# GATv2 edge scores: products on VectorE, gathers written out, turned one-hots made on ScalarE

## The reference, cut to what matters

```python
x_l = (x @ W_l + b_l).reshape(n, H, C)      # n=6250, H=8, C=32
x_r = (x @ W_r + b_r).reshape(n, H, C)
x_j = x_l[src]
g = leaky_relu(x_r[dst] + x_j, 0.2)
alpha = einsum('ehc,hc->eh', g, att) + log(edge_attr)[:, None]
# ... softmax of alpha over the edges of each dst, out = segment_sum(x_j * alpha, dst)
```

## Time and profile before

| what | value |
|---|---|
| time of three runs | 5920.71, 5924.41, 5925.23 us; median 5924.41 |
| the profiled execution | 5924.94 us, its span 5923.2 us |
| busy over the span | PE 68%, DVE 44%, ACT 19%, POOL 52% |
| granted TensorE clock, mean | 0.749 of full speed |
| HBM traffic over the span | 104 GB/s |
| `score_edges` | from about 245 to 1546 us of the span |

### The profile page before, as it was taken

The page is one execution under the profiler, slowest core; times in us unless marked ns, Lnnn a source line. Parts: engine busy times, 40 slices in busy tenths (PEclk is TensorE's granted clock), DMA queues, the critical chain, the costliest instruction groups (busy, mean ns, idle before and its releaser), DMA issues. The chain is left out here.

```text
span 5923.2 us, 82263 instructions
## 1 busy us (share of the span) xinstructions
PE 4048.7 (68%) x19460; PEld 3300.3 (56%) x19461; DVE 2628.5 (44%) x5923; ACT 1112.7 (19%) x2524; POOL 3097.9 (52%) x3161
## 2 busy tenths in 40 slices
PE   4788999999469965089934555555455555592998
PEld 3577888888447744067734444444444444461665
DVE  5333333333689975034444434444433334342443
ACT  0122222222159921022210000000000000021121
POOL 1166767676248831500066777777677777603111
PEclk9889888888679985599955556666555555555999
DMA  5365555565248843342242111111211111122220
GB/s 197 94 183 182 180 178 181 177 181 177 70 157 273 272 135 108 122 125 64 62 122 54 32 32 33 33 33 30 44 33 32 33 32 34 28 72 81 84 79 31
DMA packets 414884, 602.72 MB, mean 102 GB/s; under 512 B 97612, under 2 KB 305118, under 8 KB 413351
## 3 DMA queue, kind: packets, MB, share of 16 engines
q1 hardware_dynamic: 283019, 348.08, 17.8%
q0 software_dynamic: 107056, 200.91, 14.7%
q10 hardware_dynamic: 24732, 52.87, 2.6%
HBM read 392.17 MB, written 221.97 MB: 104 GB/s over the span
## 5 line engine op out<-in xcount | busy, mean ns | idle before, releaser
L1867 POOL DMA_INDIRECT big<-t_d,src_tiles x1564 | 1497.9, 958 | 552.2 <-issue 462.5
L2090 PE MATMUL v_bank<-big,v_oh 128*128 x3328 | 682.9, 391 | 926.4 <-POOLq L1863 861.6
L2090 PEld LDWEIGHTS v_bank<-big,v_oh 128*128 128x128 f32 x3328 | 649.6, 299 | 1004.0 <-issue 1004.0
L640 POOL DMA_INDIRECT se_xj<-xl_d,se_idx x832 | 833.8, 1002 | 371.9 <-issue 193.0
L1945 DVE TENSOR_TENSOR big<-big,v_bank 128x64 f32 x1664 | 367.8, 221 | 1158.0 <-PE v_bank L2090 922.8
L737 PE MATMUL se_z_ps<-big,se_oht 128*128 x1664 | 543.4, 455 | 73.1 <-issue 45.7
L683 DVE TENSOR_TENSOR se_z<-se_z_ps,se_xj 128x528 f32<-128x528 f32 x416 | 293.3, 705 | 584.8 <-DMA se_xj<-xl_d,se_idx 450.3
L976 POOL TENSOR_TENSOR ae_v<-ae_v,ex 128x1792 f32<-128x1792 f32 x104 | 334.2, 3217 | 243.0 <-DMA ae_v<-xj_d 242.8
L759 PEld LDWEIGHTS se_al_ps<-atta,se_zt 128*128 128x128 f32 x3328 | 459.3, 214 | 0.0
L759 PE MATMUL se_al_ps<-atta,se_zt 128*128 128x8 f32 x3328 | 444.5, 260 | 0.0
L1017 PE MATMUL ae_bank<-ae_v,ae_oh 128*128 128x266 f32 x1664 | 401.1, 396 | 51.4 <-DVE big L1001 37.4
(11 more groups left out here) (406 smaller groups left out, 5916.6 us busy)
## 6 DMA issues: line engine op xcount, KB each, us to landing
xj_d<-se_xj SPq DMA_DIRECT2D x208, 528.0 KB, 3.4
ae_v<-xj_d SPq DMA_DIRECT2D x208, 528.0 KB
big<-t_d,src_tiles POOLq DMA_INDIRECT x1564
buf_d<-e_blank ACTq DMA_DIRECT2D x4, 4112.0 KB, 35.7
e_xs<-buf_d SPq DMA_DIRECT2D x106, 128.0 KB
y_d<-e_y SPq DMA_DIRECT2D x106, 128.0 KB
se_xj<-xl_d,se_idx POOLq DMA_INDIRECT x832, 3.1
v_xt<-xnt_d SPq DMA_DIRECT2D x98, 128.0 KB
```

Of the source, the lines that this page charges most:

```text
L640: nc.gpsimd.indirect_dma_start(half_of(u)[:, k, :], None, table, bass.IndirectOffsetOnAxis(ap=idx[:, u, k:k + 1], axis=0)).then_inc(landed ...
L1867: nc.gpsimd.indirect_dma_start(rows[:, t % RING, :], None, table, bass.IndirectOffsetOnAxis(ap=m.srct[:, t:t + 1], axis=0)).then_inc(lande ...
L2090: last = nc.tensor.matmul(bank[u][:, k * MH:(k + 1) * MH], oh[:, u, k, :], of_block(rows, at[k]), start=True, stop=True)
```

## The change

In `score_edges`:

- The gathers are written out: 832 instructions without a loop. Each reads its column of `m.src` itself; the copy into `idx` and the wait on it are gone. The half buffers are now a part of `m.big1`.
- PE only expands (L738 in the changed file). Turning the one-hot, turning the sum and the product with `m.atta` are gone, and `z_ps` has four buffers.
- DVE, for each pair, adds the rows (L685, as before), then computes max(z, 0) times 0.8 att in one instruction (L693, `weigh`; `attb` holds 0.8 att on each partition), and sums each 32 channels into `m.ex` (L698, `total`). Once a group it adds the linear part (L708). `project_nodes` makes `attl` with 0.2 in place of 0.6, since leaky_relu(z) is also 0.2 z + 0.8 max(z, 0).
- The turned one-hot is made directly: `edge_steps` copies `fl` to bfloat16 and stores it to DRAM (`dlr_d`), SP loads a group's 1024 destinations as one row broadcast to all partitions (`dlb`, 256 KB in SBUF), and ACT computes 1 - |destination - partition|, cut at 0, in two instructions of 128x1024 (L722, L724).

```diff
@@ edge_steps @@
-                sp.wait_ge(stored, 112)
+                sp.wait_ge(floats, 4)
+                sp.dma_start(m.dlr_d.rearrange("(j p) e -> p j e", p=P), flb[:, :, :]).then_inc(stored, 16)
+                sp.wait_ge(stored, 128)
...
+                dve.wait_ge(floats, 3)
+                nc.vector.tensor_copy(flb[:, :, :], fl[:, :, :]).then_inc(floats, 1)
@@ score_edges, POOL @@
-                    if at_least(h, 4):
+                for h in range(2 * NG):
+                    u, r = h % 4, h // 4
+                    if h >= 4:
                         pool.wait_ge(landed[u], 16 * HS * r)
                         pool.wait_ge(s["z_ready"], 2 * h - 6)
                         pool.wait_ge(stored[u], 16 * r)
-                    nc.gpsimd.tensor_copy(idx[:, u, :], m.src[:, bass.ds(h * HS, HS)]).then_inc(s["indexed"], 1)
-                    pool.wait_ge(s["indexed"], h + 1)
-                    pool.sem_inc(s["issued"], 1)
                     for k in range(HS):
+                        t = h * HS + k
                         nc.gpsimd.indirect_dma_start(half_of(u)[:, k, :], None, table,
-                                                     bass.IndirectOffsetOnAxis(ap=idx[:, u, k:k + 1], axis=0)).then_inc(landed[u], 16)
-                pipeline(pool, 2 * NG, 4, (0, gather))
+                                                     bass.IndirectOffsetOnAxis(ap=m.src[:, t:t + 1], axis=0)).then_inc(landed[u], 16)
@@ score_edges, SP @@
+                def load_locals(h, u, r):
+                    if u % 2:
+                        return
+                    g = 2 * r + u // 2
+                    if at_least(h, 4):
+                        sp.wait_ge(s["oh_apart"], g - 1)
+                    sp.dma_start(dlb[:, u // 2, :], m.dlr_d[bass.ds(g * GS, GS), :].rearrange("k e -> (k e)").partition_broadcast(P))\
+                        .then_inc(locals_in[u // 2], 16)
-                pipeline(sp, 2 * NG, 4, (0, store))
+                pipeline(sp, 2 * NG, 4, (0, load_locals), (4, store))
@@ score_edges, DVE @@
-                    nc.vector.tensor_tensor(z[:, u, k:k + 2, :], z_ps[v % 2][:, :, 0:LW], xj[:, u, k:k + 2, :],
+                    nc.vector.tensor_tensor(z[:, u, k:k + 2, :], z_ps[v % 4][:, :, 0:LW], xj[:, u, k:k + 2, :],
                                             ALU.add).then_inc(s["z_ready"], 1)
+                def weigh(q, v, r):
+                    u, k = v // GP, 2 * (v % GP)
+                    dve.wait_ge(s["z_ready"], q + 1)
+                    if at_least(q, 2):
+                        dve.wait_ge(s["totalled"], q - 1)
+                    nc.vector.scalar_tensor_tensor(w[:, v % 2, :, :], z[:, u, k:k + 2, 0:D], 0.0, wide,
+                                                   ALU.max, ALU.mult).then_inc(s["weighed"], 1)
+
+                def total(q, v, r):
+                    dve.wait_ge(s["weighed"], q + 1)
+                    nc.vector.tensor_reduce(m.ex[:, bass.ds(q * 2 * H, 2 * H)],
+                                            w[:, v % 2, :, :].rearrange("p k (h c) -> p (k h) c", h=H), AX.X, ALU.add)\
+                        .then_inc(s["totalled"], 1)
-                pipeline(dve, NS // 2, 2 * GP, (7, scores), (0, one_hot), (3, add))
+                pipeline(dve, NS // 2, 2 * GP, (0, add), (1, weigh), (2, total), (3, scores))
@@ score_edges, ACT @@
+                def spread(g, u, r):
+                    act.wait_ge(locals_in[u], 16 * (r + 1))
+                    if at_least(g, 2):
+                        act.wait_ge(s["z_made"], GP * (g - 1))
+                    row = oht[:, u, :, :].rearrange("p k n -> p (k n)")
+                    nc.scalar.activation(row, dlb[:, u, :], ACT.Abs, bias=place[:, 0:1], scale=-1.0).then_inc(s["oh_apart"], 1)
+                    act.wait_ge(s["oh_apart"], g + 1)
+                    nc.scalar.activation(row, row, ACT.Relu, bias=m.ones[:, 0:1], scale=-1.0).then_inc(s["oht_ready"], 1)
@@ score_edges, PE @@
-                pipeline(pe, NS // 2, 2 * GP, (0, turn_one_hot), (2, expand), (4, turn), (6, attend))
+                pipeline(pe, NS // 2, 2 * GP, (0, expand))
```

More of the change, by code:

```diff
@@ L609, in score_edges @@
         HS = GS // 2
-        idx = sb("idx", [P, 4, HS], U32)
-        xj = sb("xj", [P, 2, GS, LW])
+        xj = m.big1[:, CL:CL + 2 * GS * LW].rearrange("p (u k d) -> p u k d", u=2, k=GS)
         half_of = lambda u: xj[:, u // 2, (u % 2) * HS:(u % 2 + 1) * HS, :]
-        oh, identb = sb("oh", [P, 2, GS, P], BF16), sb("identb", [P, P], BF16)
+        dlb, place = sb("dlb", [P, 2, GS * P], BF16), sb("place", [P, 1])
         oht = sb("oht", [P, 2, GS, P])
         z = sb("z", [P, 2, GS, LW])
[L617 to L621, removed]
+        w = sb("w", [P, 2, 2, D])
+        attb = sb("attb", [P, D])
+        z_ps = [ps(f"z_ps{i}", [P, 2, 512]) for i in range(4)]
         s = {n: m.sem("se_" + n) for n in
-             "indexed issued xj0 xj1 xj2 xj3 st0 st1 st2 st3 oh_ready oht_made oht_ready z_made z_ready zt_made zt_ready att_made al_ready keys".split()}
+             "xj0 xj1 xj2 xj3 st0 st1 st2 st3 att_in att_scaled dl0 dl1 placed oh_apart oht_ready z_made z_ready weighed totalled al_ready keys".split()}
+        locals_in = [s["dl0"], s["dl1"]]
         landed, stored = [s[f"xj{u}"] for u in range(4)], [s[f"st{u}"] for u in range(4)]
@@ L661, in _ @@
             def _(dve):
[L662 to L671, removed]
+                dve.wait_ge(s["att_in"], 16)
+                nc.vector.tensor_scalar(attb[:, :], attb[:, :], 1 - SLOPE, None, ALU.mult).then_inc(s["att_scaled"], 1)
+                dve.wait_ge(s["att_scaled"], 1)
+                wide = attb[:, :].unsqueeze(1).to_broadcast([P, 2, D])
                 def add(q, v, r):
@@ L689, in scores @@
                     u, g = v // GP, 2 * r + v // GP
[L690 to L694, removed]
-                pipeline(dve, NS // 2, 2 * GP, (7, scores), (0, one_hot), (3, add))
+                    dve.wait_ge(s["totalled"], q + 1)
@@ L697, in _ @@
+                    ex = m.ex[:, bass.ds(g * GS * H, GS * H)].rearrange("p (k h) -> p k h", h=H)
+                    nc.vector.tensor_tensor(ex, ex, z[:, u, :, D:LW], ALU.add).then_inc(s["al_ready"], 1)
+                pipeline(dve, NS // 2, 2 * GP, (0, add), (1, weigh), (2, total), (3, scores))
             @block.scalar
             def _(act):
[L699 to L704, removed]
-                        act.wait_ge(s["z_made"], GP * (g - 1))
-                    nc.scalar.copy(oht[:, u, 4 * half:4 * half + 4, :].rearrange("p k n -> p (k n)"), oht_ps[:, :]).then_inc(s["oht_ready"], 1)
@@ L708, in absolute @@
[L708 to L713, removed]
+                act.dma_start(attb[:, :], a["L0_gnn_att"].rearrange("h c -> (h c)").partition_broadcast(P)).then_inc(s["att_in"], 16)
@@ L715, in _ @@
+                pipeline(act, NG, 2, (0, spread))
             @block.tensor
             def _(pe):
[L717 to L726, removed]
@@ L731, in expand @@
                     g = 2 * r + v // GP
-                    pe.wait_ge(s["oht_ready"], 2 * g + (v % GP) // 2 + 1)
-                    if at_least(q, 2):
-                        pe.wait_ge(s["z_ready"], q - 1)
+                    pe.wait_ge(s["oht_ready"], g + 1)
+                    if at_least(q, 4):
+                        pe.wait_ge(s["z_ready"], q - 3)
                     blocks = blocks_of(nc, m, mybir.EngineType.PE, q * 2, 2)
                     for i in range(2):
-                        last = nc.tensor.matmul(z_ps[v % 2][:, i, 0:LW], oht[:, u, k + i, :], of_block(m.xr, blocks[i]),
+                        last = nc.tensor.matmul(z_ps[v % 4][:, i, 0:LW], oht[:, u, k + i, :], of_block(m.xr, blocks[i]),
                                                 start=True, stop=True)
                     last.then_inc(s["z_made"], 1)
[L741 to L762, removed]
-                pipeline(pe, NS // 2, 2 * GP, (0, turn_one_hot), (2, expand), (4, turn), (6, attend))
+                pipeline(pe, NS // 2, 2 * GP, (0, expand))
 def normalise_edges(nc, m, a):
```

13 lines of the change are left out of this document (6 added, 7 removed).

## The result

The changed kernel takes **5757.41 us** (median of 4 runs, 5754.34 to 5764.05) where the kernel before took 5924.82 (4 runs beside it): ratio 0.9723, 95% interval 0.9706 to 0.974. The forecast was 5815, its range 5736 to 5915, and "faster" had 0.84.

What follows compares the result with a forecast made beforehand. POOL's stream of gathers, stretched by DVE, was taken as the scoring stage's bound. 204 halves x (6.015 - 5.46) save 113 us; 5924.9 - 113 + 3 + 5 - 5 = 5815 us, range 5736 to 5915.

Steps and rivals of the forecast that it cites:

- What bounds: Scoring stage: POOL's stream of gathers, stretched by DVE, sets the pace at 6.015 us a half; PE does not.
- Gathers without copy: POOL, scoring stage: without copy and wait, four gathers at the convolution's 1.274 us each, 5.10 us a half.
- The holds: Scoring gathers starting during a weigh end late: 0.40 us in three quarters of halves, 0.58 more in one of ten.
- The second reckoning: Scoring stage: if gathers met weighs at random, 0.087 us lost a gather, 0.35 us a half.
- the addition of `z` holds nothing: DVE, scoring stage: this addition reads one operand from PSUM, so it was taken as harmless to gathers.
- The edges: Outside the steady halves: edge table's store +3 us, scoring start +5, scoring end -5.
- The bfloat16 copy: DVE in `edge_steps`: at most 1.11 us, hidden in the 1.21 us that DVE idles.
- The sum: Whole kernel: 113 us saved over 204 halves, edges +3, +5 and -5, from 5924.9 to 5815 us.
- B: Rival, scoring stage: the weigh costs gathers nothing; 5.10 us a half, 187 us saved, 5741 us; chance 0.16.
- C: Rival, scoring stage: both weighs hold a gather in each half; 6.08 us a half, 5941 us; chance 0.12.
- D: Rival, scoring stage: PE's block-number loads make it the pace; 6.4 us a half, 87 us lost, 6015; chance 0.05.
- The signs: Scoring profile if right: gaps 0.30 us, about 735 gathers in 1000 us, mean near 1.04, one in four near 1.3.

Runs made afterwards that it cites:

- the second: The unmodified changed kernel measured once more beside the kernel before: 5765.37 us (4 runs) against 5924.93, ratio 0.9728.

## Why the prediction was right, point by point

- **What bounds.** Right. POOL's gathers did, and what PE shed was worth nothing: the gathers alone gave all (5757.0).
- **Gathers without copy, 5.10 a half.** Right in kind, 0.09 too dear. The convolution's rows carried stalls of 2.07 us into the sum; the new scoring has not one in 832 gathers, while the convolution, whose code is of the same form, keeps its own in every run. Bare halves take 5.01 (attention row in PSUM). The reason that the prediction gave for the stalls, that written-out code is fetched, is not borne out: the loop of before has them without one transfer of instructions, the written-out gathers have the transfers and no stall. What makes them is open.
- **The holds, 0.36 a half.** The mechanism was right, the size not. Taking the holds away gave 5.251 - 5.013 = 0.24 a half, 49 us. The prediction put the add 2.03 us behind the half's last gather, so that the third gather was hit in most halves. In the changed kernel that distance is 3.26 in the median (2.17 to 4.40 from the 5th to the 95th percentile), and the 148 held gathers spread over the four places (63, 43, 10, 32). Neither part of the change does that alone: with the gathers alone the distance stayed at 2.13 at nearly the same pace, with the new scoring alone at 2.23 at the old pace, both at a DMA share of 0.67; together the share is 0.78. That the fuller queues make the adds late fits this but is not shown, since the one run made to test it, without the loads of destinations, was disturbed. The second reckoning, by random meetings (0.35), was high for another reason, here reckoned anew: a gather lasts 0.95 us anyway and a hold ends 0.82 behind the weighing, so the first 0.13 us cost nothing. 4 x (0.68 - 0.13) of the 10.5 us of a group is 0.21 of the gathers, at 0.28 each: 0.23 a half, as measured. That the addition of `z` holds nothing was right too, but the prediction's reading of the earlier trace rows could not show it: the gather of 815.31 had ended before the addition of 816.33 began. The trace of before does, with 226 gathers that start inside such an addition, none of them over 1.0 us.
- **The edges.** The bfloat16 copy (0.63 us) hid: DVE's pause before the next evacuation fell from 1.21 to 0.55. The edge table's stage grew by 6.0 in this pair and by 2.4 in the second, for an estimate of 3. The start cost 9.4, not 5: the mechanism as told. The end gave 3.9 of 5.
- **The sum.** Against the profiled execution (5764.05) the forecast was 51 us high: 204 x (5.46 - 5.23) = 47 are the two terms of the half, the three edges took back 8, and the other stages, which the change hardly touches, gave 11. That execution lies 6.6 over the median.
- **The rivals.** B gave 5741, near the time, for a wrong reason: the weighing isn't free, it costs the 49 us between 5765 and 5716. The remark of the Trainium skill (SBUF — State Buffer, Who interferes with whom) that `tensor_tensor` does not stall the making of descriptors is contradicted here: all 94 held gathers of the kernel before end 0.82 to 0.83 us behind the one-hot of L669, a `tensor_tensor`, and the rule above it on the same page, two SBUF operands, parts the cases rightly (148 held against none). The fourth gather of a half was held in 32 of 203 halves, but two gathers in one half, as C wants it, in 18. D did not come at all: DVE waited 69.5 us for PE in the whole stage, 59.6 of them at its start. D's sum was also wrong by itself: at 6.4 a half, 204 x 0.385 is 79 us lost and 6006 in all, not 87 and 6015; the forecast did not use it.
- **The signs.** The gaps were 0.30 throughout and 755 gathers came in 984 us, where the prediction had 735 in 1000. The mean gather was 1.00 us, not 1.04, and 18% of them were long, not one in four, which is the smaller hold again.

## What to carry to other kernels

When one engine's stream sets the pace, read the gap between two of its instructions at every place in the period: 0.71 us at one place in four, 204 times, is 145 of the 155 us here, and the large redesign beside it gave nothing by itself. (Whether the old scoring, with an operand of its one-hot in PSUM and the keys late, would also reach 5676 us was not run.) In these runs a DVE instruction with two SBUF operands holds a gather that starts while it runs until 0.82 us behind its own end; putting the constant operand in PSUM removed that. Loads needed late (3.3 MB of keys) belong behind the first small ones that start the pipeline: 48 us here.

## What was not expected of the hardware

- With more work put before it PE got more clock: 0.88 with 5405 matmuls in 900 us, 1.00 with 6150, at 824 and 822 us busy, and 0.75 with 1380. A PE busy for 92% had at least 14% in hand.
- The stalls of 2.0 us in POOL's stream came every 157 to 159 us with the index copy, in a loop or not, and mostly every 143 us in the convolution; never in 832 gathers of the changed kernel. They do not go with transfers of instructions.
- The same program, the gathers alone, took 5757 us in one run and 6513 in four others, and the sign of the edit changed with it (before took 5925 and 6414, ratios 0.972 and 1.016): a ratio holds for the conditions in which it was measured.
